# Gated mix plus long convolution on one core: out rows in halves of the time, one DMA issue per out store

## What is computed

```python
def _L0_cond_ref(x, condition, weights):
    W = weights[condition]
    return jnp.einsum('bct,bcd->bdt', x, W)

def _L1_cond_ref(u, log_dt, C, log_A_real, A_imag, D, length):
    K = _get_kernel(log_dt, C, log_A_real, A_imag, Lq)
    n = 2 * Lq
    y = jnp.fft.irfft(jnp.fft.rfft(u, n=n) * jnp.fft.rfft(K, n=n)[None], n=n)[..., :Lq]
    y = y + u * D[:, None]
    mask = (jnp.arange(Lq)[None, :] < length[:, None]).astype(u.dtype)
    return y * mask[:, None, :]

x = x + _L0_cond_ref(x, itok_B_0_15, L0_cond_weights)
x = x + _L1_cond_ref(x, ..., itok_B_78_3631)
```

## Time and profile before

| what | value |
|---|---|
| median of 3 runs | 1099.62 us (1095.68 to 1100.15) |
| the profiled execution's own time | 1099.54 us |
| its span, first to last instruction | 1097.7 us |
| busy in the span: TensorE, VectorE, ScalarE, GpSimd | 91%, 70%, 50%, 46% |
| DMA | 305.48 MB, mean 278 GB/s |
| mean granted TensorE clock | 0.984 of full speed |

### The profile page before, as it was taken

How to read it: one execution, slowest core, us unless ns; L and a number is a source line. 1 busy time by engine, 2 the same in 40 slices (tenths; PEclk the granted TensorE clock), 3 DMA queues, 4 the chain that set the end, 5 groups by cost and what they waited for, 6 DMA issues and landing times.

```text
span 1097.7 us, 29010 instructions
## 1 busy us (share of the span) xinstructions
PE 996.0 (91%) x11526; PEld 731.3 (67%) x11526; DVE 770.1 (70%) x1710; ACT 547.3 (50%) x1163; POOL 502.4 (46%) x542
## 2 busy tenths in 40 slices
PE   6987789677756999999999999999999999999997
PEld 2332244232224788888888888888888888888886
DVE  6989920000004888888888888888888888888885
ACT  2633344334332555555555555555555555555553
POOL 2111043000204466656656656556666566565530
PEclk9999999999997999999999999999999999999999
DMA  9999999999989899999999999999999999999994
GB/s 334 415 425 421 425 421 423 376 424 424 423 320 312 179 220 249 228 218 234 215 234 230 222 238 225 221 232 218 239 229 226 235 230 229 226 226 234 221 214 117
DMA packets 220311, 305.48 MB, mean 278 GB/s; under 512 B 79938, under 2 KB 178626, under 8 KB 211986
## 3 DMA queue, kind: packets, MB, share of 16 engines
q1 hardware_dynamic: 219490, 302.37, 97.6%
q10 hardware_dynamic: 528, 1.05, 0.4%
q0 software_dynamic: 160, 0.20, 0.1%
HBM read 152.37 MB, written 134.41 MB: 261 GB/s over the span
## 4 chain that ended last, share of the span: by engine, by line
PE 67%; DMA 25%; ACT 4%; SPq 2%; issue 1%; DVE 1%; ACTq 0%
DMA u_scratch<-stage 24%; PE bank L479 15%; PE bank L488 15%; PE bank L444 13%; PE bank L430 10%; PE bank L456 7%; PE bank L485 5%; ACT stage L554 3%; PE bank L418 2%; DVE x_t L831 1%; DMA x_f<-in_x 1%; SPq L248 1%; SPq L215 0%; SPq L235 0%; DVE st_sb L821 0%
## 5 line engine op out<-in xcount | busy, mean ns | idle before, releaser
L479 PE MATMUL bank<-toep,u_t 128*128 128x192 f16 (+1 forms) x3072 | 344.7, 220 | 0.4
L816 DVE SCALAR_TENSOR_TENSOR u_t<-bank,u_t 128x512 f16<-128x512 f32 x256 | 176.3, 688 | 193.9 <-ACT u_t L567 191.8
L488 PE MATMUL bank<-g_sb,st_sb 128*128 128x256 f16 x1536 | 307.4, 274 | 0.0
L418 PE MATMUL bank<-x_f,w_buf 128*128 128x512 f32 x512 | 240.7, 618 | 64.1 <-ACT stage L554 52.7
L430 PE MATMUL bank<-ident,u_row 128*128 128x128 f32 x1024 | 280.9, 279 | 11.7 <-DMA u_row<-u_scratch 11.1
L575 ACT ACTIVATE st_sb<-bank 128x128 f16<-128x128 f32 x448 | 123.8, 276 | 289.2 <-PE bank L456 199.5
L479 PEld LDWEIGHTS bank<-toep,u_t 128*128 128x128 f16 x3072 | 232.0, 99 | 14.9 <-issue 0.4
L418 PEld LDWEIGHTS bank<-x_f,w_buf 128*128 128x128 f32 x512 | 95.8, 195 | 204.7 <-issue 110.6
L846 DVE COPY_PREDICATED o_sb<-mask,u_row 128x512 f32<-128x512 uint8 x256 | 205.7, 803 | 16.6 <-issue 16.6
L554 ACT ACTIVATE stage<-bank 128x1024 f32<-128x1024 f32 x128 | 123.9, 1021 | 174.0 <-DMA u_scratch<-stage 156.8
L485 PE MATMUL bank<-toep,x_t 128*128 128x64 f16 x2048 | 189.0, 193 | 0.3 <-issue 0.3
(11 more groups left out here) (122 smaller groups left out, 842.9 us busy)
## 6 DMA issues: line engine op xcount, KB each, us to landing
x_f<-in_x SPq DMA_DIRECT2D x64, 1024.0 KB, 19.6
u_row<-u_scratch SPq DMA_DIRECT2D x128, 512.0 KB, 5.8
out<-o_sb SPq DMA_DIRECT2D x256, 256.0 KB, 4.0
u_scratch<-stage SPq DMA_DIRECT2D x60, 1024.0 KB, 17.7
toep<-k_scratch SPq DMA_DIRECT2D x64, 256.0 KB, 5.6
u_scratch<-stage SPq DMA_DIRECT2D x4, 896.0 KB, 10.2
gt_sb<-g_sb SPq DMA_TRANSPOSE x128, 5.3
u_scratch<-stage SPq DMA_DIRECT2D x4, 128.0 KB, 4.7
```

The source lines that it names most:

```text
L418: last = pe.matmul(bank[:, 4 * (n % 2) + k, :], w_buf[n % XS][:, :], x_f[n % XS][:, k * 512:(k + 1) * 512], start=True, stop=True)
L479: pe.matmul(bank[:, y, col + tb * P + NM:col + Q], u[:, h, tb, a, rows_], t[:, h, b, NM:Q - tb * P], start=first, stop=False, skip_group_c ...
L488: last = pe.matmul(bank[:, y, col:col + Q], st[:, h, a, gr * ROWS:(gr + 1) * ROWS], g[:, h, b, :], start=False, stop=(m == 2), skip_group_ ...
L816: dve.scalar_tensor_tensor(out=t[:, q // 2, q % 2, 1, :], in0=bank[:, 4 + q, :], scalar=US, in1=t[:, q // 2, q % 2, 0, :], op0=MUL, op1=SU ...
```

## The change

Chunk `j` now belongs to set `j // 4` and group `j % 4`: a row holds half of the time, and is one run of 4 KB in the out row. A table function `at(j)` gives the column at which chunk `j` lies in the state tiles. The evacuation of the first stage, the offsets of the mask and the waits on the states in `out_part` follow. `store_out` issues one DMA of 512 KB in place of two of 256 KB, and the waits on `s_store` count 16 per store in place of 32.

```diff
+        def at(j):
+            return (j % NG * JJ + j // NG) * NB
+
         def state(t, part, j):
-            return ap(t, part * NG * ROWS + j * NB, [[2 * NG * ROWS, 2], [1, NB]])
+            return ap(t, part * NG * ROWS + at(j), [[2 * NG * ROWS, 2], [1, NB]])
 
         def new_state(j):
-            return bank[:, 0:2, (j - 1) * NB:j * NB]
+            return bank[:, 0:2, at(j - 1):at(j - 1) + NB]
...
             def store_out(i, c, h):
                 o = 2 * (c % 2) + h
                 sp.wait_ge(s_ov, 4 * (UN * i + c) + 2 * h + 2)
-                for j in range(JJ):
-                    dst = bass.AP(out.tensor, (2 * (UN * i + c) + h) * T + j * Q,
-                                  [[H * T, NB], [JJ * Q, NG], [1, Q]])
-                    sp.dma_start(dst, o_sb[o][j * NB:(j + 1) * NB, :, :]).then_inc(s_store[o], 16)
+                dst = bass.AP(out.tensor, (2 * (UN * i + c) + h) * T, [[NG * Q, JJ], [H * T, NB], [1, NG * Q]])
+                sp.dma_start(dst, o_sb[o][:, :, :].rearrange("p g t -> p (g t)")).then_inc(s_store[o], 16)
...
             for o in range(4):
-                sp.wait_ge(s_store[o], 32 * (PAIRS // 2))
+                sp.wait_ge(s_store[o], 16 * (PAIRS // 2))
...
-            do(pool.iota(row_i[:, :], pattern=[[0, 1]], base=0, channel_multiplier=Q // NB))
+            do(pool.iota(row_i[:, :], pattern=[[0, 1]], base=0, channel_multiplier=NG * Q // NB))
...
-                        last = pe.matmul(bank[:, h, j * NB:(j + 1) * NB],
+                        last = pe.matmul(bank[:, h, at(j):at(j) + NB],
                                          lam_sb[c % 2][:, h, a, :, :].rearrange("p k m -> p (k m)"),
-                                         st_sb[c % 2][:, h, b, j * NB:(j + 1) * NB], start=False, stop=(m == 2),
+                                         st_sb[c % 2][:, h, b, at(j):at(j) + NB], start=False, stop=(m == 2),
...
                 if h == 0:
-                    pe.wait_ge(s_sth, 7 * n + JJ * gr + 1)
-                    pe.wait_ge(s_stl, 7 * n + JJ * gr + 1)
+                    pe.wait_ge(s_sth, 7 * n + NG + gr)
+                    pe.wait_ge(s_stl, 7 * n + NG + gr)
...
-                mixed = bank[:, 4 * (n % 2):4 * (n % 2) + 4, :].rearrange("p a (j b t) -> p j a b t", b=2, t=P)
                 for j in range(JJ):
-                    act.activation(stage[n % STAGES][:, j, :, :].rearrange("p a (b t) -> p a b t", t=P),
-                                   mixed[:, j, :, :, ::-1], ACT.Copy).then_inc(s_ev, 1)
+                    half = bank[:, 4 * (n % 2) + 2 * j:4 * (n % 2) + 2 * j + 2, :]
+                    act.activation(stage[n % STAGES][:, j, :, :].rearrange("p a (b t) -> p (a b) t", t=P),
+                                   half.rearrange("p a (b t) -> p (a b) t", t=P)[:, :, ::-1], ACT.Copy)\
+                        .then_inc(s_ev, 1)
...
-                    act.wait_ge(s_store[o], 32 * (UN // 2 * i + c // 2))
+                    act.wait_ge(s_store[o], 16 * (UN // 2 * i + c // 2))
...
-            ts(row_i[:, :], row_i[:, :], Q, None, ALU.bitwise_and)
+            ts(row_i[:, :], row_i[:, :], NG * Q, None, ALU.bitwise_and)
...
-                ts(len_f[:, g:g + 1], len_f[:, NG:NG + 1], float(-g * JJ * Q), None, ADD)
+                ts(len_f[:, g:g + 1], len_f[:, NG:NG + 1], float(-g * Q), None, ADD)
```

## The result

The changed kernel takes 1923.98 us (median of 4 runs, 1914.18 to 1926.92) against 1097.73 us before (4 runs). The ratio is 1.7495, with a 95% interval of 1.7441 to 1.7548. The profiled execution took 1926.92 us, with a span of 1925.1 us.

A forecast was written before the change was run, and what follows sets the result against it. DMA engines bound the mixing, TensorE the convolution. First store at 364.4 us, plus 1285 for stores, 415 for other transfers and about 2 for landing gave 2066, with 1.8 around it 2068 us; range 1829 to 2230 us.

The forecast's parts named there:

- The mechanism: Out stores: slowest dimension 2 puts each store on two of 16 DMA engines; 166,498 packets in SP's queue.
- The mapping at no cost: Evacuations, mask, state tiles and `out_part` waits: new chunk order costs 0, at most 1.5 us per pair.
- The store at 10.04 us: Out stores: 262,144 bytes per engine at 26.1 GB/s, 10.04 us each; 128 stores give 1285 us.
- The slower bound of 16.8 us: Out stores: one engine's time per store if runs cost as in the stores before the change.
- The 9.0 us named beside the sum: Out stores: time per store at the skill page's 29 GB/s per engine; the sum would be about 130 us lower.
- The rest at 6.8 us: A pair's u_row, toep and gt transfers on the same two engines: 6.8 us, for 61 pairs 415 us.
- The bound by bytes alone, 3.8 us: A pair's other transfers on the two engines: lower bound, 1.57 MB at 418 GB/s.
- The ends: Start and end of the store stage: first store at 364.4 us, about 2 us for the last landing.
- Rival 2 (gaps): SP's queue, held at transposing DMAs, leaves two engines waiting: 250 us more, 2318 us; chance 0.12.
- Rival 1 (16 engines): Out stores keep 16 engines and nothing is slower: 1099 us; chance 0.07.
- Its threshold, 9 engines or more: Out stores: a pair's DMA work stays within TensorE's 11.6 us only with 9 or more engines.
- The signs named ahead: Changed profile: convolution DMA share below 0.4, about 98 GB/s, TensorE share some 0.43, store landing 20 us or more.

The follow-up runs named there:

- run 3: The changed kernel with batch elements reordered in the partitions and two DMAs per store, slowest dimension 8: 1122.42 us, ratio 1.0232 to the kernel before.
- run 4: The changed kernel with batch elements reordered and two DMAs per store, slowest dimension 4: 1340.62 us, ratio 1.2186 to the kernel before.
- run 5: The changed kernel with batch elements reordered and two DMAs per store, slowest dimension 2: 1946.9 us, ratio 1.7705 to the kernel before.
- run 8: The kernel before, old mapping and 1 KB runs, with each store of 64 batch elements issued as 62 and 2: 2025.94 us, ratio 1.8424.
- run 6: The changed kernel without the transposing DMAs after the first two pairs: 1837.39 us, ratio 1.6709 to the kernel before.
- run 1: The changed kernel's mapping and 4 KB runs, each store as two DMAs of 64x1024, one per set: 1103.87 us against 1099.61 for the kernel before.
- run 10: The changed kernel with two DMAs of 64x1024 per store, to rows 512 KB apart instead of the right places: 1093.87 us, ratio 0.9934 to the kernel before.

## Why the prediction was right, and where its sizes were off

**The mechanism: right.** The count of packets of a 256 byte load had said that a transfer is cut by its slowest dimensions. The changed kernel has exactly the 166,498 packets named, and runs 3, 4, 5 and 8 show the rule at 8, 4, 2 and 62. The rule of the Trainium skill, DMA: Bandwidth & Descriptors, section "Why a DMA increments its semaphore by 16 and not by 1", held in each of them. The count was thin, as it rested on one load of 1 x 64 elements, which is no test of a dimension of 2. But it was sound: run 6 has 124 fewer transposing DMAs and 166,498 - 99,042 = 67,456 = 124 x 544 fewer packets, the 544 that the prediction had left for each.

```profile
q1 hardware_dynamic: 99042, 286.09, 41.4%
```

**The mapping at no cost:** right. Run 1 is 0.4% slower, some 4 us, but in run 10, with the same mapping and the rows elsewhere, TensorE is busy for 690 of the 694 us as before and the kernel is 0.7% faster. So the 4 us belong to the stores and not to TensorE's columns or waits.

**The store at 10.04 us: 9.9 us,** from 53 GB/s on two engines at the end; 128 stores give 18 us less than predicted. The slower bound of 16.8 us, read off spread stores in 1 KB runs, was no price of a lone engine: by the 48 GB/s of run 8 such a store takes 10.9 us. The 9.0 us named beside the sum were too low.

**The rest at 6.8 us: 4.4 us** (24.23 - 19.8). This is the term that was mis-sized, and it makes 61 x 2.4 = 146 us less. The parts measured add up to 4.7: u_row 2.5, transposes 1.34 and toep 0.87 us. The prediction had read 6.6 out of the DMA share between 1061 and 1070 us, taken 6.8 without giving a reason for the step, and used the share of 1.01 in the convolution for its upper end. Run 6 shows what that share holds: open packets of the transposes. So that the DMA engines were "occupied nearly always" before was not shown by it either. The bound by bytes alone, 3.8 us, was nearer.

**The ends: more.** The sum had 2 us for the last landing. The measured span is 1925 us, where 364 + 128 x 9.9 + 61 x 4.4 is 1900: about 25 us lie at the start and end of the stage. The runs don't divide them further. All three together turn 2066 into 1925. That the time came out within 8% owes something to luck: the ends took back 23 of the 164 us by which the other two terms were too high.

**Rival 2 (gaps): out at its size.** It asked for 250 us; taking out all transposes but the first four saved 87 us, gaps and packets together. What there is of gaps is inside the transposes' 1.34 us. SP needed 5.5 us for each transposing DMA, but a held-up SP meant a full queue nearly always, as was argued. **Rival 1 (16 engines)** was out with the packet count. Its threshold, 9 engines or more, was roughly right by luck: with 4.4 us for the rest and 26.5 GB/s for each engine six would have been enough by the sum, but eight still cost 2.3%, as eight engines did not reach eight times the rate of one.

**The signs named ahead.** The rate in the convolution was to be 98 GB/s and is 107, as the pair is shorter; its 24.23 us lie within the 23 to 29 named. TensorE was to idle more than half the time, with a busy share of 0.43; it is 954 / 1486 = 0.64. It is busy for 15.6 us per pair in place of 11.5, at a granted clock of 0.80 in the mean: after a wait of 3.7 us for u_row that ended at 1004.7 us, for instance, it had 0.50, the lower level of 1.2 GHz, from 1006 to 1009 us. The mean DMA share was to be below 0.4 and is 0.83, for the reason found in run 6. The landing of the stores is not shown for such transfers; that of the loads shows it in its place.

## What to carry to other kernels

Before you join two DMAs into one, look at the slowest dimension of both sides as the instruction carries it. In every run here the largest number up to 16 that divides both was the number of engines. A 2 there left 53 GB/s where 16 engines move 418 in the mixing, for that transfer, and it delayed all that stood behind it. Count packets against runs in the profile (runs plus one per engine) to see how many engines a transfer has. And don't take the DMA share for work where transposing DMAs are in flight: bytes at the rate of one engine gave the better price.

## What the runs showed of the hardware

- One engine stores 4 KB runs at 26.5 GB/s when two or four engines carry the stores (53 and 105 GB/s); eight carried 170 GB/s in run 3.
- On two engines a 1 KB run takes 43 ns, against 39 ns for its bytes in 4 KB runs (48 GB/s in run 8, 53 in the change).
- Two transposing DMAs of 128 KB each cost the two busy engines 1.34 us per pair, 2.2 times the 0.6 us of their bytes, with near-stops of some 0.9 us in a third of the pairs; the toep load in 512 B runs costs 0.87 us, about 1.4 times its bytes.
- Without the transposes the DMA share fell from 0.83 to 0.29 at nearly the same rate.
- With stores to rows 512 KB apart the kernel took 1% less than with the same stores in their places, 1 MB apart (1093.87 against 1103.87 us), at the same number of engines and issues.
